# Weight set-up in pieces beside the first groups' stages, and order lists of their own for the filling and emptying steps

## The chip, the cores and the metric

One core of one Trainium2 chip. The metric is the time of one execution on the device in microseconds (us). Every time below is of the kernel before, from its runs or from one profiled execution of it.

## The reference

128 graphs of 64 nodes with 256 features pass four layers, each followed by a residual sum and a layer norm. With `x` the running features and `adj` the adjacency of a graph:

```python
# layer 0: hypergraph convolution, twice (W1: 256 -> 512, W2: 512 -> 256)
H = (adj != 0); w = adj[first row]
conv(x, W, b) = 1/(H @ w) * (H @ (1/colsum(H) * (H.T @ (x @ W.T)))) + b
h = layer_norm(relu(conv(x, W1, b1)), gamma, beta)
x = LN(x + conv(h, W2, b2) + x)
# layer 1: q, k = split(x @ Wqk1); w = rowsum(q * (adj @ (k * mask))) / 16
x = LN(x + softmax(w * mask over nodes) * (x @ Wv1))
# layer 2: 8 heads of 32, scores * (adj + adj), softmax, Wo, biases
x = LN(x + attention(x; Wq, bq, Wk, bk, Wv, bv, Wo, bo))
# layer 3: gate = sigmoid(rowsum(adj) * Wd + bd); xg = x * gate
QK = sigmoid(xg @ Wqk3.T + bqk); s = QK @ QK.T / 16 * adj; a = s / rowsum(s)
x = LN(x + relu((a @ xg) @ Wl.T + bl + xg @ Wr.T))
```

## The kernel before, in words

The 8192 rows of `x` are cut into 32 groups of 256 (4 graphs, two tiles of 128 rows). Every product with a float32 operand is made from two float16 parts, high and low, by three matmuls (`mm3`, lines 460 to 462: hi·hi, hi·lo, lo·hi). ScalarE (ACT) casts the high part, VectorE (DVE, `low`, line 898) or GpSimd (POOL, `sub`, line 1202) makes the low part by subtraction.

**The pipeline.** The work on a group is cut into six streams, `stream0` to `stream5` on each engine: 0 and 1 are layer 0, 1 and 2 layer 1, 2 to 4 layer 2, 4 and 5 layer 3. In step s, stream k works on group s − k. There are 37 steps: steps 0 to 5 fill the pipeline (written out), steps 6 to 31 have all six streams (a loop of two steps a turn), steps 32 to 36 empty it (written out). Each stream is a Python generator that yields after each piece of work. `run` (lines 271 to 289) takes, for each engine, one list written out by hand or by a planner (`ORDER_PE`, `ORDER_ACT`, `ORDER_DVE`, `ORDER_POOL`, lines 44 to 47): entry k lets stream k emit its next piece. So a list is the fixed order in which one engine does the pieces of the six streams in a step; engines wait for each other only by semaphores, and each does its own list strictly in order. In filling and emptying steps the same list is used, and entries of streams that have no group are skipped.

**Names of pieces** used below, with the lines of the matmuls or instructions. PE: `wt` (turn of the layer 1 weights, 595), `W2a` and `W2b` (the product with W2 for tile 0, last piece of stream 0, and for tile 1, first of stream 1), `md` (hypergraph matrix and degree, 519 to 525), `z1`, `zA`, `zB` (product with W1 in two halves), `rsum` (sums for the layer norm, 556 to 560), `conv2`, `x1t`, `x2t`, `xgt` (turns of x1, x2, xg, 485), `u` (product with Gm), `k`, `v`, `q`, `sc0`, `sc1` (scores, 638), `et0`, `et1` (turns of the exponentials, 649), `ctx0`, `ctx1` (662), `o` (product with Wo), `qk3`, `y3`, `s3`, `o2`, `rowsum` (706, 707), `o1` (layer 3). DVE: `HT` (964) and `cnt` (967) begin stream 0, `HBh`, `HBl`, `Pl`, `z1l`, `rFl1` (1006), `rmean`, `rmm`, `rvar` (1009 to 1015) end it; `y0` (1023), `Sm1`, `mx1` (1104, 1109), `SA` (1159), `preF` (1137), `stF` (954), `ssum` (1169), `o3` (1179). ACT: `xC`, `xF` (norms, 739), `exp0`. POOL: `xl`, `y0l` (1202), `preG` (1312), `xg` (1301). In the trace `late` is the name of two large buffers that hold the staged weights first, then x3, x4, Sm, Ssb, cx, gw, xg, o2 and o3.

**The set-up.** Before any stream begins, the eleven weights are loaded, split and partly combined: SyncE (SP) issues W2, the twelve small inputs, W1 and the nine other weights, and after them the first group's `x` and adjacency (`load_conv`, `load_layer1`), one queue in order. DVE clears its buffers, waits for W2 and all small inputs, scales W2 by gamma, centres it by column sums from PE, and makes the low parts of all eleven weights; ACT casts the high parts; PE makes two sums over W2, the product Gm of the two halves of Wqk1, and bv·Wo, and then waits until all eleven are split (`unstaged`) before its first stream piece. The eleven weights are staged in `late0`, `late1`, `r` and `rsq`.

```python
            pe.wait_ge(ev("unstaged"), len(weights_in))   # PE, ahead of its streams
...
            pool.wait_ge(ev("unstaged"), len(weights_in)) # POOL, ahead of its streams
...
            def step(j, s, lo, hi):
                live = {k: streams[k](At(k, j, s)) for k in range(lo, hi + 1)}
                for k in order:
                    if k in live:
                        next(live[k], None)
```

PSUM banks are held from piece to piece: stream 0 works in bA (from `md` to the sums; the next group's `md` waits for `rvar`), layer 3 in bG (from `xgt` to `o1`; the next `xgt` waits for `o3`).

Of the kernel before, what the change touches and what calls it, by code (L numbers as in the profile page):

```python
# [43 lines left out]
ORDER_PE = [2, 1, 4, 3, 5, 0, 4, 2, 3, 2, 0, 5, 1, 4, 0, 2, 5, 3, 0, 0, 3, 1, 5, 4, 5, 1, 5, 3, 2, 3, 1, 0, 2, 0, 4]  # L44
ORDER_ACT = [0, 4, 3, 1, 5, 2, 0, 5, 0, 3, 5, 4, 0, 4, 4, 5, 1, 0, 0, 0, 1, 0, 0, 0, 3, 2, 1, 3, 2, 5, 4, 3, 2, 4, 5]
ORDER_DVE = [0, 0, 4, 0, 0, 2, 0, 2, 0, 1, 0, 4, 0, 4, 0, 4, 3, 5, 4, 0, 2, 2, 1, 5, 1, 3, 1, 0, 2, 5, 2, 3, 2, 4, 3, 3, 3, 1, 5, 0, 4, 5, 4, 5, 4, 1, 5, 2, 3, 1, 5, 5, 0, 1, 0, 3, 2, 4, 0]
ORDER_POOL = [0, 0, 0, 1, 1, 0, 4, 3, 1, 1, 1, 1, 5, 2, 2, 3, 2, 0, 3, 0, 4, 0, 4, 4, 5, 4, 5, 5, 5, 0, 0, 0]
# [4 lines left out]


def build(nc, x, adj, adj_t, mask, mask_col, w1t, b1, gamma, beta, w2t, b2, wqk1t, wv1, wqt, bq, wkt, bk, wvt, bv,
          wot, bo, wqk3t, bqk, wlt, bl, wrt, wd, bd, out):
    ctx = ExitStack()
    with ctx:
# [28 lines left out]
        def weight(name, chunks, n):  # L86
# [28 lines left out]
                  "Wqk3": r[:, 0:2], "Wl": r[:, 2:4], "Wr": rsq[:, 0:2]}  # L115
# [103 lines left out]
        g2 = sb("g2", [P, TILES, D])  # L219
        xgFh = sb("xgFh", [P, 2, TOK], F16)  # L220
# [88 lines left out]
        def _(sp):  # L309
# [82 lines left out]
            def stage_in(i):  # L392
# [4 lines left out]
            small = [(gam[:], gamma), (bet[:], beta),  # L397
                     (wdb[:], wd.rearrange("(o d) -> o d", o=1).broadcast_to([P, D])),
# [958 lines left out]
```

## Time and profile before

| what | us |
|---|---|
| median of 3 runs | 1034.5 |
| lowest, highest run | 1030.52, 1379.15 |
| the profiled execution | 1032.15 |
| its span, first to last instruction | 1030.4 |
| mean granted TensorE clock in it (share of full) | 0.962 |

The span is a little shorter than the execution's time; what is between them, 1.75 us, lies outside the instructions. One run of the three was 1379.15 us; the other two and the profiled execution lie within 4 us of each other.

### The profile page before, as it was taken

Reading aid. Unit: us, or ns where it says so; the run is one execution under the profiler, and the core shown is the slowest. Engines: PE = TensorE matmul, PEld = TensorE weight load, DVE = VectorE, ACT = ScalarE, POOL = GpSimd, SP = SyncE. Lnnn points to the kernel's source line nnn. Section 1 sums busy time; section 2 is a strip of 40 time slices with the busy share of each in tenths; the row PEclk is TensorE's granted clock in tenths of the full one; section 3 lists DMA queues with packets and bytes.
Section 4 is the critical chain, followed back from the end, with each engine's and each line's share of the span. In section 5 each row is a group of like instructions: output and inputs, shape, how many; then the busy total and the mean of one; then the engine's idle time right before and its main releaser. Section 6 shows DMA issues by size and latency. Waiting matters only on the chain.

```text
span 1030.4 us, 32446 instructions
## 1 busy us (share of the span) xinstructions
PE 939.0 (91%) x11228; PEld 817.9 (79%) x11228; DVE 851.3 (83%) x2503; ACT 723.2 (70%) x1516; POOL 753.2 (73%) x1163
## 2 busy tenths in 40 slices
PE   3477899999999999999999999999999999998854
PEld 2356778888888888888888888888888888887642
DVE  4335789999999999999999999999999999987742
ACT  2234577787777787777877777887777777776542
POOL 3245678888888888888888888888888888875541
PEclk9579999999999999999999999999999999999975
DMA  7100222222222222222222221222222222211100
GB/s 212 32 27 8 59 60 62 71 71 69 68 56 66 55 58 56 67 59 69 69 69 66 56 65 53 57 59 69 59 69 69 69 64 62 53 45 39 49 14 20
DMA packets 110231, 61.80 MB, mean 60 GB/s; under 512 B 57072, under 2 KB 105840, under 8 KB 110192
## 3 DMA queue, kind: packets, MB, share of 16 engines
q1 hardware_dynamic: 110192, 61.30, 22.8%
q8 instruction: 22, 0.36, 0.1%
q14 instruction: 17, 0.14, 0.0%
HBM read 35.83 MB, written 8.39 MB: 43 GB/s over the span
## 4 chain that ended last, share of the span: by engine, by line
PE 72%; DVE 17%; ACT 4%; POOL 2%; issue 2%; DMA 1%; SPq 1%; POOLq 0%; ACTq 0%; DVEq 0%
PE bank L460 19%; PE bank L462 17%; PE bank L461 17%; PE bank L638 4%; PE bank L485 4%; DVE rFl L1006 4%; PE bank L662 3%; PE bank L649 2%; DVE Smx L1109 2%; DVE late L1104 2%; DVE late L1164 2%; DVE preF L1137 2%; DVE x1Fl L898 1%; PE bank L560 1%; PE bank L530 1%
## 5 line engine op out<-in xcount | busy, mean ns | idle before, releaser
L460 PE MATMUL bank<-z1h,W 128*128 128x256 f16 x256 | 71.7, 280 | 3.4 <-DVE z1l L898 3.3
L461 PE MATMUL bank<-z1l,W 128*128 128x256 f16 x256 | 71.4, 279 | 0.0
L462 PE MATMUL bank<-z1h,W 128*128 128x256 f16 x256 | 71.4, 279 | 0.0
L461 PE MATMUL bank<-W,rFh 128*128 128x256 f16 x256 | 71.0, 277 | 0.0
L462 PE MATMUL bank<-W,rFl 128*128 128x256 f16 x256 | 71.0, 277 | 0.0
L460 PE MATMUL bank<-W,rFh 128*128 128x256 f16 x256 | 70.9, 277 | 0.0
L1289 POOL TENSOR_TENSOR late<-late,Smx 128x512 f32<-128x512 f32 x64 | 67.8, 1060 | 2.4 <-DVE Smx L1109 1.7
L766 ACT ACTIVATE r<-bank,b1c 128x256 f32<-128x256 f32 x128 | 52.7, 465 | 8.7 <-PE bank L462 7.5
L1219 POOL TENSOR_TENSOR gp<-late,bdb 128x512 f32<-128x512 f32 x32 | 52.8, 1650 | 6.2 <-ACT late L846 6.2
L1104 DVE TENSOR_TENSOR late<-bank,acD 128x512 f32<-128x512 f32 x64 | 43.8, 684 | 14.7 <-PE bank L638 14.6
L1244 POOL TENSOR_TENSOR rsq<-rsq 128x512 f32<-128x512 f32 x32 | 52.8, 1650 | 2.2 <-ACT rsq L774 2.2
L1150 DVE SCALAR_TENSOR_TENSOR Ql<-qt,Qh 128x512 f16<-128x512 f32 x32 | 35.6, 1111 | 20.9 <-ACT Qh L873 20.7
L1202 POOL TENSOR_TENSOR rFl<-r,rFh 128x512 f16<-128x512 f32 x32 | 37.2, 1162 | 19.2 <-ACT rFh L723 19.2
L739 ACT ACTIVATE late<-preG,nbG,rsG 128x256 f32<-128x256 f32 x64 | 35.0, 594 | 21.9 <-POOL nbG L1214 21.9
L485 PE MATMUL bank<-ident,late 128*128 128x128 f32 x256 | 40.5, 282 | 10.6 <-POOL late L1301 10.4
L1006 DVE TENSOR_TENSOR rFl<-r,rFh 128x512 f16<-128x512 f32 x32 | 43.4, 1357 | 8.1 <-ACT rFh L723 8.1
L638 PE MATMUL bank<-Kbd,qh 128*64 128x256 f16 x512 | 46.9, 278 | 2.4 <-DMA Kbd<-kst 2.4
L1207 POOL TENSOR_SCALAR veB<-mvB 128x2 f32<-128x2 f32 x32 | 7.0, 219 | 54.7 <-DVE mvB L959 54.7
L723 ACT ACTIVATE SAh<-SA 128x256 f16<-128x256 f32 x32 | 13.4, 417 | 47.2 <-DVE SA L1159 47.1
L835 ACT ACTIVATE E<-late 128x512 f32<-128x512 f32 x64 | 39.9, 623 | 8.7 <-POOL late L1289 8.7
L739 ACT ACTIVATE late<-preF,nbF,rsF 128x256 f32<-128x256 f32 x64 | 35.0, 593 | 15.3 <-POOL nbF L1214 15.1
L954 DVE BATCH_NORM_STATS2 stG<-preG 128x6 f32<-128x256 f32 x64 | 24.1, 419 | 25.6 <-POOL preG L1312 25.6
(286 smaller groups left out, 4625.9 us busy)
## 6 DMA issues: line engine op xcount, KB each, us to landing
Vbd<-vst SPq DMA_DIRECT2D x128, 66.0 KB, 2.1
xin<-x SPq DMA_DIRECT2D x32, 256.0 KB, 2.7
xres<-x SPq DMA_DIRECT2D x32, 256.0 KB, 2.8
Kbd<-kst SPq DMA_DIRECT2D x128, 64.0 KB, 2.0
out<-late SPq DMA_DIRECT2D x32, 256.0 KB, 2.2
mrow<-mask SPq DMA_DIRECT2D x32, 128.0 KB, 3.1
atA<-adj_t SPq DMA_DIRECT2D x64, 32.0 KB, 2.3
aC<-adj SPq DMA_DIRECT2D x64, 32.0 KB, 2.1
```

The costliest lines, as they stand in the source:

```text
L460: pe.matmul(o, sh, mh, start=start, stop=False, skip_group_check=True)
L461: pe.matmul(o, sh, ml, start=False, stop=False, skip_group_check=True)
L462: return pe.matmul(o, sl, mh, start=False, stop=stop, skip_group_check=True)
L485: m = pe.transpose(o[:, c * TOK + t * P:c * TOK + (t + 1) * P], src[:, t, c * P:(c + 1) * P], ident_[:])
L638: m = pe.matmul(o[64 * b:64 * b + 64, c * 256:(c + 1) * 256], qq[:, c, tok], Kbd[:, :, hl, c, tok], start=(i == 0), stop=(i == 2), skip_gr ...
L739: m = act.activation(dst[:, t], pre[k][:, t], ACT.Identity, bias=nb[k][:, t:t + 1], scale=rs[k][:, t:t + 1])
L766: m = act.activation(r[:, 2 * i + c], (bA, bB)[i][:, c * TOK:(c + 1) * TOK], ACT.Relu, bias=b1c[:, 2 * i + c:2 * i + c + 1], scale=1.0 / WS)
L1006: dve.tensor_tensor(rFl[:, 2:4], r[:, 2:4], rFh[:, 2:4], ALU.subtract).then_inc(ev("rF_lo1"), 1)
L1104: dve.tensor_tensor(Sm[:, t], (bD0, bD1)[t][:].rearrange("p (h k) -> p h k", h=HEADS), acD[:, at.par, t:t + 1].broadcast_to([P, HEADS, NOD ...
L1219: return pool.tensor_tensor(dst, src, b[:].rearrange("p (o d) -> p o d", o=1).broadcast_to([P, TILES, D]), ALU.add)
L1244: pool.tensor_tensor(rsq[:, 0:2], rsq[:, 0:2], rsq[:, 2:4], ALU.add).then_inc(ev("sq_sum"), 1)
L1289: pool.tensor_tensor(Ssb[:, t], Sm[:, t], Smx[:, t:t + 1].rearrange("p t h -> p h t").broadcast_to([P, HEADS, NODES]), ALU.subtract).then_ ...
```

## The change

The set-up becomes a seventh stream (number 6, `set_up` on each engine), whose pieces stand in the lists of steps 0 to 3. Steps 0 to 5 and 32 to 36 get lists of their own (`HEAD_*`, `TAIL_*`); the lists of the loop (`ORDER_*`) are changed too. SP issues W1, the first group's `x` and adjacency, gamma, beta, b1, W2, Wqk1 and Wv1, the other small inputs, the first group's layer 1 inputs, and then the seven other weights. The general waits ahead of the streams go; each piece that needs a weight waits for that weight's count of `unstaged`, for group 0 alone. Wqk3, Wl and Wr are staged in gp, gt and o3r, the sums over W2 go to banks bF0 and bF1 and bv·Wo to bG. The clearing of Kbd, Vbd and vst on POOL is cut into nine pieces.

In names of pieces (S for a set-up piece; `Sx` on ACT and DVE is the high or low part of weight x), the lists that the text below speaks of; "was" is what the old list leaves of itself in that step:

```text
PE   loop  was  wt W2b ctx0 k qk3 md ctx1 wback v wsum Pt y3 conv2 cxt z1 v1 s3 sc0 zA zB sc1 x1t o2 o rowsum u o1 et0 x2t et1 uxT rsum q W2a xgt
           now  k wt W2b qk3 md wback ctx0 ctx1 v wsum y3 conv2 Pt v1 z1 cxt sc0 s3 zA zB sc1 x1t o2 o rowsum u et0 x2t o1 et1 uxT rsum q W2a xgt
PE   step 0 was md Pt z1 zA zB rsum W2a
           now  md Pt z1 zA zB S(sum) S(beta) S(Gm) rsum W2a
DVE  step 0 was HT cnt cnt1 be HBh HBl Dbg Dd Dinv Pl z1l rFl1 rmean rmm rvar
           now  HT cnt cnt1 be HBh HBl Dbg Dd Dinv Pl S(copy) S(scale) SW1 z1l S(beta) S(centre) S(c2) rFl1 SW2 rmean S(small) rmm rvar
ACT  step 1 was xh y0h Pf Ph z1h xB relu0 relu1 rFh0 x1Fh sq0 rFh1 sq1 uh
           now  SW2 xh y0h Pf SGm SWv1 Ph SWq z1h xB relu0 relu1 rFh0 x1Fh sq0 rFh1 sq1 uh
DVE  loop  was  ... mx1 x1Fl o2 rFl1 preF ssum stF srec mvF ul o3 ...
           now  ... mx1 x1Fl o2 preF rFl1 stF ssum mvF srec ul o3 ...
PE   step 35 was ctx0 qk3 ctx1 y3 cxt s3 o2 o rowsum o1 xgt
           now  ctx0 ctx1 qk3 cxt y3 o s3 o2 rowsum o1 xgt
DVE  step 35 was deg ri0 cx0 ri1 Ql cx1 y3l SA cFl o2 preF ssum stF srec mvF o3 stG mvG xgFl
           now  deg ri0 cx0 ri1 cx1 cFl Ql y3l preF SA stF mvF o2 ssum srec o3 stG mvG xgFl
POOL step 35 was gp SAl veF rsF nbF preG xg veG rsG nbG
           now  gp veF SAl rsF nbF xg preG veG rsG nbG
```

```diff
+HEAD_PE = [[0, 0, 0, 0, 0, 6, 6, 6, 0, 0], [1, 0, 0, 1, 0, 0, 0, 1, 1, 1, 0, 0], ...
...
+SETUP = LAST_LAG + 1
...
             def step(j, s, lo, hi, order):
                 live = {k: streams[k](At(k, j, s)) for k in range(lo, hi + 1)}
+                if j is None and s <= LAST_LAG:
+                    live[SETUP] = pieces
                 for k in order:
-                    if k in live:
-                        next(live[k], None)
+                    next(live[k], None)
...
             for s in range(first):
-                step(None, s, 0, s)
+                step(None, s, 0, s, head[s])
...
             for s in range(last, STEPS):
-                step(None, s, max(0, s - GROUPS + 1), LAST_LAG)
+                step(None, s, max(0, s - GROUPS + 1), LAST_LAG, tail[s - last])
...
-            stage_in(1)
+            stage_in(0)
+            sp.wait_ge(ev("const"), 2)
+            load_conv(At(0, None, 0))
+            for dst, src in ((gam[:], gamma), (bet[:], beta), (b1c[:], b1)):
+                sp.dma_start(dst, src).then_inc(ev("w2_in"), 16)
+            stage_in(1)
+            for i in range(2, 4):
+                stage_in(i)
             for dst, src in small:
                 sp.dma_start(dst, src).then_inc(ev("small_in"), 16)
-            stage_in(0)
-            for i in range(2, len(weights_in)):
+            load_layer1(At(0, None, 0))
+            for i in range(4, len(weights_in)):
                 stage_in(i)
-            sp.wait_ge(ev("cleared"), 1)
-            load_conv(At(0, None, 0))
-            load_layer1(At(0, None, 0))
...
-            pe.wait_ge(ev("unstaged"), len(weights_in))
+            pe.wait_ge(ev("ident"), 3)
+
+            def set_up():
+                pe.wait_ge(ev("setup"), 2)
+                for k in range(4):
+                    m = pe.matmul(bF0[:, 0:D], onesf[:], w2_stage[:, k, 0:D], start=(k == 0), stop=(k == 3))
+                m.then_inc(ev("setup_pe"), 1)
+                yield
...
+            def first_needs(at, k):
+
+                if not at.earlier(1):
+                    pe.wait_ge(ev("unstaged"), k)
...
+            dve.memset(atA[:], 0.0).then_inc(ev("const"), 1)
+            dve.memset(aC[:], 0.0).then_inc(ev("const"), 1)
...
+                dve.wait_ge(ev("w2_in"), 64)
+                dve.tensor_copy(w2_stage[:, :, D:2 * D], w2_stage[:, :, 0:D]).then_inc(ev("setup"), 1)
...
-            for part, value in ((Kbd[:], 0.0), (Vbd[:], 0.0), (vst[:, 1], 0.0), (vst[:, 0], 1.0)):
-                pool.memset(part, value).then_inc(ev("ident"), 1)
-            pool.wait_ge(ev("unstaged"), len(weights_in))
+            def set_up():
+                for h in range(4):
+                    pool.memset(Kbd[:, h], 0.0).then_inc(ev("ident"), 1)
+                    yield
...
```

## Rows read from the trace of the kernel before

**Rows 1.** The page: PE busy, then its busy tenths in 40 slices

```profile
PE 939.0 (91%) x11228; PEld 817.9 (79%) x11228; DVE 851.3 (83%) x2503; ACT 723.2 (70%) x1516; POOL 753.2 (73%) x1163
...
PE   3477899999999999999999999999999999998854
```

**Rows 2.** Windows, one a step: length, busy us by engine, PEclk, DMA

```profile
29.22:50.44 21.22, 9.41 (x71) 7.18 (x72) 5.50 (x18) 5.88 (x13) 4.71 (x8) 0.58 0.15 38
50.44:75.67 25.23, 17.89 (x130) 13.09 (x128) 9.15 (x31) 8.57 (x18) 10.55 (x18) 0.70 0.09 27
75.67:99.12 23.45, 18.31 (x170) 14.69 (x169) 12.84 (x45) 10.82 (x24) 12.09 (x22) 0.93 0.04 10
99.12:123.77 24.65, 20.69 (x226) 17.02 (x225) 17.81 (x53) 14.28 (x31) 15.73 (x25) 1.00 0.25 61
123.77:150.26 26.49, 24.86 (x316) 20.58 (x316) 22.12 (x66) 18.05 (x39) 19.69 (x31) 1.00 0.23 59
...
178.69:207.08 28.39, 28.19 (x361) 25.05 (x354) 26.06 (x77) 22.27 (x49) 23.43 (x37) 1.00 0.26 65
907.30:934.58 27.28, 25.17 (x300) 21.94 (x300) 22.73 (x64) 17.26 (x34) 19.30 (x31) 0.94 0.15 38
...
977.84:997.78 19.94, 13.11 (x134) 9.97 (x134) 9.92 (x27) 10.04 (x19) 7.29 (x13) 0.83 0.06 18
```

**Rows 3.** DMA issues to 60 us: count, KB each, median us to landing

```profile
late<-w2t SPq DMA_DIRECT2D x1, 512.0 KB, 4.0
late<-w1t SPq DMA_DIRECT2D x1, 512.0 KB, 6.3
...
atA<-adj_t SPq DMA_DIRECT2D x8, 32.0 KB, 3.0
```

**Rows 4.** Timeline of DVE: start, us, instruction, [idle before <-releaser]

```profile
12.64 0.69 DVE L922 COPY late<-late 128x1024 f32<-128x1024 f32 x1 [9.34 <-DMA bvc<-bv]
...
17.01 1.23 DVE L898 SCALAR_TENSOR_TENSOR W<-late,W 128x1024 f16<-128x1024 f32 x1 [1.30 <-ACT W L723]
...
28.90 0.29 DVE L964 TENSOR_SCALAR HT<-atA 128x256 f16<-128x256 f32 x1
...
37.74 0.69 DVE L898 SCALAR_TENSOR_TENSOR z1l<-bank,z1h 128x512 f16<-128x512 f32 x1 [2.18 <-ACT z1h L723]
...
54.80 0.88 DVE L1023 SCALAR_TENSOR_TENSOR y<-bank,rsc,c 128x256 f32<-128x256 f32 x2 [2.43 <-PE bank L462]
```

**Rows 5.** Timeline of PE, set-up and around the end of step 0

```profile
17.98 1.89 PE L496 MATMUL bank<-late,betb 128*128 128x256 f32 x8
...
48.19 0.16 PE L556 MATMUL bank<-ones,rFh 128*128 128x1 f16 x1 [5.36 <-POOL rsq L1247]
...
49.48 0.37 PE L460 MATMUL bank<-W,rFh 128*128 128x256 f16 x1
...
54.34 0.42 PE L462 MATMUL bank<-W,rFl 128*128 128x256 f16 x1
```

**Rows 6.** Timeline of POOL, set-up

```profile
1.57 3.51 POOL L1198 MEMSET Kbd<- 128x4096 f16 x1
```

**Rows 7.** Waits of PE in the loop (170 to 850 us): total, times, longest

```profile
PE bank L460 <- DVE ssum L1169: 2.3, 11, 0.2
```

**Rows 8.** Timeline of ACT in one step of the loop

```profile
225.35 1.08 ACT L739 ACTIVATE x<-preC,nbC,rsC 128x256 f32<-128x256 f32 x2
```

**Rows 9.** Timeline of DVE in the same step

```profile
226.69 0.14 DVE L1169 TENSOR_SCALAR ssum<-bank 128x2 f32<-128x2 f32 x1
226.81 0.75 DVE L954 BATCH_NORM_STATS2 stF<-preF 128x6 f32<-128x256 f32 x2
```

**Rows 10.** Timeline of DVE in step 35

```profile
997.17 0.69 DVE L1137 SCALAR_TENSOR_TENSOR preF<-bank,x2b 128x512 f32<-128x512 f32 x1 [0.62 <-PE bank L462]
...
998.98 0.88 DVE L1179 SCALAR_TENSOR_TENSOR late<-bank,srec,late 128x256 f32<-128x256 f32 x2
```

**Rows 11.** Timeline of POOL in step 35

```profile
1002.21 1.26 POOL L1301 TENSOR_TENSOR late<-g,late 128x512 f32<-128x512 f32 x1
```

More of the change, by code:

```diff
@@ L219, in build @@
         g2 = sb("g2", [P, TILES, D])
+        for name, buf in (("Wqk3", gp), ("Wl", gt), ("Wr", o3r)):
+            stages[name] = buf[:]
         xgFh = sb("xgFh", [P, 2, TOK], F16)
@@ L762, in stream0 @@
                     act.wait_ge(ev("y0_raw"), at.n(-1))
+                if not at.earlier(1):
+                    act.wait_ge(ev("w2_in"), 64)
                 def relu(i):
@@ L824, in stream3 @@
                 yield
+                if not at.earlier(1):
+                    act.wait_ge(ev("ident"), 13)
                 act.wait_ge(ev("v"), at.n())
@@ L843, in stream4 @@
             def stream4(at):
+                if not at.earlier(1):
+                    act.wait_ge(ev("small_in"), 16 * SMALL_INPUTS)
                 act.wait_ge(ev("deg"), at.n())
@@ L851, in stream4 @@
                 yield
+                if not at.earlier(1):
+                    act.wait_ge(ev("unstaged"), len(weights_in))
                 act.wait_ge(ev("gate_pre"), at.n())
@@ L1092, in stream3 @@
             def stream3(at):
+                if not at.earlier(1):
+                    dve.wait_ge(ev("ident"), 13)
                 dve.wait_ge(ev("k_hi"), at.n())
@@ L1196, in _, with set_up @@
             pool.wait_ge(ev("ident"), 3)
-            for part, value in ((Kbd[:], 0.0), (Vbd[:], 0.0), (vst[:, 1], 0.0), (vst[:, 0], 1.0)):
-                pool.memset(part, value).then_inc(ev("ident"), 1)
-            pool.wait_ge(ev("unstaged"), len(weights_in))
+            def set_up():
+                for h in range(4):
+                    pool.memset(Kbd[:, h], 0.0).then_inc(ev("ident"), 1)
+                    yield
+                for par in range(2):
+                    for b in range(2):
+                        pool.memset(Vbd[:, par, b], 0.0).then_inc(ev("ident"), 1)
+                        yield
+                for part, value in ((vst[:, 1], 0.0), (vst[:, 0], 1.0)):
+                    pool.memset(part, value).then_inc(ev("ident"), 1)
+                yield
             def sub(dst, a, b):
@@ L1259, in stream1 @@
             def stream1(at):
+                if not at.earlier(1):
+                    pool.wait_ge(ev("setup"), 5)
                 pool.wait_ge(ev(f"xres_in{at.par}"), at.dma(1))
@@ L1281, in stream3 @@
                     pool.wait_ge(ev("preF"), at.n(-2))
+                if not at.earlier(1):
+                    pool.wait_ge(ev("unstaged"), 8)
                 pool.wait_ge(ev("xC"), at.n())
@@ L1293, in stream4 @@
             def stream4(at):
+                if not at.earlier(1):
+                    pool.wait_ge(ev("unstaged"), 9)
                 pool.wait_ge(ev("gate_scaled"), at.n())
```

194 lines of the change are left out of this document (116 added, 78 removed).

## The prediction

> **What bounds the kernel now.** I read the page first, then windows of one step each, then the timelines of the stretches where the windows show idle time. The page has PE busy 939.0 of 1030.4 us, and its 40 slices show where it is not: the first four and the last five [rows 1]. The windows put sizes to this [rows 2]. Their bounds are the starts of `cnt` (DVE), once a step, and at the end those of `ssum`. A step of the loop takes 28.39 us with PE busy 28.19: 26 such steps, 738 us, are bound by PE, and no order can give back more than 0.2 × 26 = 5.2 us there. The filling steps 0 to 4 take 21.22, 25.23, 23.45, 24.65 and 26.49 us with PE busy 9.41, 17.89, 18.31, 20.69 and 24.86; they are chains of small pieces, each engine waiting for another. The emptying steps are alike: 27.28 us with 25.17 busy in step 32, 19.94 with 13.11 in step 35. Ahead of all this the first `HT` starts at 28.90 us [rows 4]: by then the whole set-up has been done and no group's work but one cast of `x`.
>
> **The start.** In the new order W1 is issued first, at the time at which W2 is now, 0.74 us; W2 landed 4.0 us after its issue [rows 3], so W1 is there at 4.7. SP then waits for two memsets that end by about 1.8 us and issues `x` (some 0.5 us) and two adjacency blocks (some 0.65 each), the last by 3.8; such blocks land 3.0 us after issue [rows 3], at 6.8. `HT` starts there in place of 28.90 [rows 4]: −22.1 us. Bounds: if the block lands as late after issue as W1 does now under load, 6.3 us [rows 3], it is 10.1 and the gain 18.8; on the other side issues half a us quicker than I count give 22.6.
> The trace shows one load of 512 KB taking 4.0 us on an idle queue and 6.3 on a full one [rows 3]. The Trainium skill (DMA: Bandwidth & Descriptors, Queues, rings and completion order) says that a transfer's semaphore write lands only after every earlier write of the same DMA engine. By that rule the group's blocks come after all of W1, which speaks against putting W1 ahead of them; here it would hold `HT` to W1's landing, and by the row for an idle queue that is already past at 4.7.
>
> **Step 0 with set-up pieces in it.** DVE now sits idle 2.18 us ahead of `z1l` [rows 4]. Three pieces go there: the copy (0.69), the scaling (about 1.1) and W1's low part (1.23) [rows 4], about 3.0 us: `z1l` comes 0.8 late, and with it `zA`, `zB`. W2 must have landed when the copy starts, 37.74 − 2.18 − 22.1 = 13.5 us; it is issued at about 5.5 and lands 4.0 to 6.3 later [rows 3], in time by 1.7 us or more. PE waits 5.36 us between `zB` and `rsum` [rows 5], and gets three pieces of eight matmuls; one such piece is 1.89 busy [rows 5], 5.2 to 5.7 together, which fit to 0.3 us. The scaling of small inputs ahead of `rmm` delays `rvar` by about 0.5. Cost: +1.3 us.
>
> **PE's clock.** The same pieces may bring something. In step 0 the granted clock was 0.58 in the mean and in step 1 0.70 [rows 2], that is the lower level (1.2 GHz) for most of it. `W2a` and `W2b`, 24 matmuls, ran from 49.48 to 54.34 [rows 5], 0.21 us apart, after the 5.36 us of idling; at the upper level they would be half that, −2.5 us. With PE busy in that gap I take the upper level for them. `y0` (54.80 [rows 4]) waits for `W2b`, but also for DVE's `HBl`, which is itself 1.3 late and would then be last: of −2.5 and +1.3 together there remains −1.1 us. The rest of step 1 has 36 matmuls of the same kind in its chain, worth up to −3.6 us, nothing if the clock falls back in the gaps; I take −1, nearer to nothing, as the 0.70 was granted with the same gaps.
>
> **Steps 1 to 3 with set-up pieces.** ACT gets ten casts, DVE ten pieces, POOL seven of the nine memsets (the whole of Kbd took 3.51 us [rows 6], so about 0.9 each), PE one short piece. A low part of 512 columns is 0.69 (`z1l`, the same shape [rows 4]); the cast of 512 columns is no more than a norm of as many, 1.08 [rows 8]. That is up to 11 us of ACT and 7 of DVE in three steps in which they are busy 33.7 and 39.8 of 73.3 us [rows 2]. In the idle stretches they cost nothing; where one stands ahead of a piece of the chain it costs its length. Between 0 and +7, I take +2: the casts `SGm` and `SWv1` stand between `Pf` and `Ph`, and PE's turn hides one of them.
>
> **The filling steps' own lists.** For PE, step 1 keeps its order. In steps 2 to 4 `q`, `v` and the score pieces move. PE idles 5.1, 4.0 and 1.6 us there [rows 2], 10.7 together, which bounds the gain; `cnt` to `rvar` is a chain through one bank that no list shortens. I take a third, −3.5, bounds −8 and +2.
>
> **The loop's lists.** PE waits for `ssum` ahead of `o1` (2.3 us in 11 steps of 24, 0.2 at most [rows 7]). The new list puts `et0` and `x2t` between: 0.9 us of work ahead of the wait, while DVE puts `stF` (0.75 [rows 9]) ahead of `ssum`. I take half of the bound of 5.2: −2.5 us; on the other side the next rival but one.
>
> **The emptying steps' lists.** In step 35 `preF` starts at 997.17 and `xg` ends at 1003.5, and only then can PE go on [rows 10, 11]. Now `o` stands ahead of `s3` and `preF` ahead of `SA`: about 4 us earlier; POOL does `xg` ahead of `preG`: 1.26 earlier [rows 11]. What is late next is bank bG, free when `o3` ends, 998.98 + 0.88 − about 0.7 [rows 10] = 999.2: −4.1 us. Steps 32 to 34 keep more of their order, with 2.1 us of PE idle in step 32 [rows 2]; I take 1 each. Sum −7, bounds −3 and −12. Step 36 has one stream and no order to change.
>
> **Sum.** −22.1 + 1.3 − 2.4 (W2 product; with the 1.3 this is the −1.1) − 1 + 2 − 3.5 − 2.5 − 7 = −35.2. On the profiled execution's own 1032.15 us: 997.0. That execution lies 2.35 us under the median of the three runs; I put half of it back: 998 us.
>
> **The rivals.**
> *Only the start is gained.* The pieces eat what the clock gives, and the lists move idle time without shortening a chain: −22.1 + 1.3 − 1.1 + 2 = −20, so 1012. For it: the chains of steps 0 and 1 keep their order. Against it: 4 us of step 35 can be read off piece by piece.
> *The lists bring more.* −8 in the filling steps, −5 in the loop, −11 in the emptying, −3 for the clock: 985. For it: PE's idle times are that large. Against: banks bA and bG.
> *The loop gets worse; slower than before.* `x2t` now stands ahead of `o1`, and everything behind it on PE, `o1`, `et1`, `uxT`, waits with it for `xC`. `xC` ends at 226.43 [rows 8]; `x2t` would start at about 227.05, 0.6 us later. If ACT reaches `xC` more than 0.6 us later than now, each further us costs 26. At 2.5 us late it is 1.9 × 26 = 49, so 998 + 2.5 + 49 = 1050; from 1.9 us late on the loss, 1.3 × 26 = 34 us, outweighs all that is gained. Against: the new ACT list has `xC` one piece earlier.
> *The loads don't do what the order says.* `x` and its blocks wait behind what is issued after them, and `HT` starts near 12: 1003.
>
> **Chances.** Forecast 0.55, by itself 990 to 1007; only the start 0.20; more 0.15; late loads 0.05; worse loop 0.05. A measurement of this kernel can tell about 2% from no change, here 1013.8. The first, third and fourth are faster, and of the second somewhat more than half (it lies 2 us under that bound): 0.55 + 0.15 + 0.05 + 0.12 = 0.87; within 2% 0.09; slower 0.04. The range 985 to 1013 leaves out half of the third, a third of the second and the last: under 0.2.
>
> **What would show it.** `HT` at 6.5 to 7.5 us; `z1l` near 16.4; `W2a` with matmuls 0.11 us apart and `y0` near 31.6; step lengths of steps 1 to 4 together under 99.8 − 2; the loop's step between 28.2 and 28.4; `xg` of step 35 ahead of `preG`. It is wrong if the loop's step is over 28.6, if DVE's wait ahead of the copy shows W2 landing after 13.5, or if the filling steps grow by as much as the start gained.

## The result and the profile after

The changed kernel takes 1002.55 us (median of 4 runs, 999.49 to 1005.13), the kernel before 1033.2 beside it (4 runs, the 1379.15 among them): ratio 0.9713, 95% interval 0.9672 to 0.9753, that one run left out. The forecast was 998, with 985 to 1013. The profiled execution took 999.49 us, span 997.7 (before: 1032.15 and 1030.4).

The page of the changed kernel: busy time by engine, then PE's busy tenths and its granted clock in 40 slices.

```profile
PE 928.4 (93%) x11228; PEld 812.0 (81%) x11228; DVE 836.6 (84%) x2503; ACT 702.5 (70%) x1516; POOL 746.0 (75%) x1169
...
PE   4687899999999999999999999999999999999854
...
PEclk9779999999999999999999999999999999999995
```

The first slice has work in it now, where [rows 1] had 3 tenths. The second thing to see is that PE has 10.6 us less of busy time for the same 11228 matmuls; so its busy time is not work alone, which matters below.

Windows of the changed kernel, cut as in [rows 2]: steps 0 to 4, one of the loop, then 32, 35 and 36.

```profile
6.72:29.99 23.27, 15.64 (x101) 12.31 (x102) 13.05 (x37) 6.93 (x14) 4.97 (x7) 1.00 0.77 231
29.99:53.58 23.59, 16.09 (x120) 11.83 (x118) 10.21 (x33) 9.49 (x20) 14.14 (x22) 0.71 0.10 29
53.58:78.14 24.56, 19.75 (x171) 16.20 (x170) 15.40 (x46) 14.44 (x31) 15.04 (x26) 0.87 0.04 9
78.14:104.56 26.42, 20.98 (x269) 17.81 (x269) 21.77 (x60) 14.31 (x32) 16.46 (x26) 1.00 0.23 57
104.56:131.17 26.61, 22.92 (x266) 20.08 (x259) 21.98 (x64) 17.18 (x38) 19.19 (x30) 1.00 0.24 58
...
161.58:189.47 27.89, 27.89 (x350) 24.77 (x349) 25.32 (x79) 21.03 (x46) 23.04 (x35) 1.00 0.25 66
882.77:904.50 21.73, 21.59 (x276) 19.14 (x274) 18.99 (x62) 13.78 (x30) 15.36 (x26) 1.00 0.12 33
...
949.03:966.97 17.94, 12.06 (x134) 9.41 (x134) 11.39 (x32) 10.06 (x20) 9.01 (x15) 0.90 0.07 20
966.97:986.72 19.75, 11.15 (x62) 7.17 (x62) 5.27 (x14) 5.88 (x11) 5.26 (x10) 0.65 0.04 13
```

Against [rows 2]: the loop's step is 0.5 us shorter in this window, steps 32 and 35 are 5.5 and 2.0 shorter, step 0 is 2.1 longer, and steps 1 to 4 together are 101.18 us where they were 99.82; the prediction wanted them under 97.8. Step 1 is granted 0.71 of the clock, where it was 0.70. The granted clock of step 0, 1.00, says less than it seems: the trace's clock records begin only at 22.7 us, and the matmuls ahead of that, shown below, still run at the lower level.

The span splits at three marks on DVE: the first `HT`, the first `rmean` (end of step 0's chain), and the `rmean` of steps 6 and 31. The table has this for every kernel that speaks to the lists (us; "new" names the lists that are those of the change).

```text
kernel       new lists    first HT   to rmean   rmean 0 to 6   loop step   rmean 31 to end   span
before       none          28.90      20.75       154.82        28.358        116.99        1030.4
start_only   none           6.12      22.22       156.40        28.342        112.10        1005.4
loop_old     fill, empty    6.19      21.74       153.39        28.358        111.83        1002.1
tail_old     fill, loop     5.93      22.18       151.36        27.974        120.57         999.4
head_old     loop, empty    5.98      22.50       153.21        27.974        112.17         993.2
after        all            6.38      22.55       155.67        28.047        111.93         997.7
```

The loop's column is the mean of 25 steps. A step is cut at `rmean`, which the new loop list has 2.7 us earlier in the step (23.06 us behind `cnt` where it was 25.74); with that list the filling stretch reads 2.7 us shorter and the last stretch 2.7 longer. From before to after: −22.5 at the start, +1.8, +0.85, −7.8 in the loop, −5.1 at the end, −32.7 in all.

**The start came as forecast.** DVE of the changed kernel in steps 0 and 1:

```profile
6.38 0.31 DVE L1035 TENSOR_SCALAR HT<-atA 128x256 f16<-128x256 f32 x1 [3.10 <-DMA atA<-adj_t]
...
13.20 0.68 DVE L980 COPY late<-late 128x1024 f32<-128x1024 f32 x1
...
16.11 0.68 DVE L951 SCALAR_TENSOR_TENSOR z1l<-bank,z1h 128x512 f16<-128x512 f32 x1
...
31.84 0.87 DVE L1094 SCALAR_TENSOR_TENSOR y<-bank,rsc,c 128x256 f32<-128x256 f32 x2
```

`HT` was forecast at 6.8 (the block's landing, which is 6.27 in the trace), `z1l` at 16.4, `y0` at 31.6. The copy of W2 starts at 13.20 with no wait for its load. PE of the changed kernel, from `zB` to W2's product:

```profile
21.59 0.42 PE L482 MATMUL bank<-z1l,W 128*128 128x256 f16 x1
21.80 0.42 PE L483 MATMUL bank<-z1h,W 128*128 128x256 f16 x1
22.01 2.21 PE L516 MATMUL bank<-late,onesf 128*128 128x256 f32 x8
24.07 1.89 PE L521 MATMUL bank<-late,betb 128*128 128x256 f32 x8
25.79 1.89 PE L527 MATMUL bank<-late 128*128 128x256 f32 x8
...
28.79 0.28 PE L481 MATMUL bank<-W,rFh 128*128 128x256 f16 x1
28.91 0.27 PE L482 MATMUL bank<-W,rFh 128*128 128x256 f16 x1
29.01 0.27 PE L483 MATMUL bank<-W,rFl 128*128 128x256 f16 x1
```

The three set-up pieces fill what was a gap of 5.36 us [rows 5]. Ahead of them matmuls start 0.21 us apart, behind them 0.11: the lower level (1.2 GHz) has given way to the upper (2.4 GHz) once PE was busy without a gap, as forecast. It did not last: in step 1 the granted clock is 0.71 again.

**The loop gained more than was thought possible.** PE around `o1`; first the kernel before:

```profile
226.50 0.27 PE L462 MATMUL bank<-x1Fh,Gm 128*128 128x256 f16 x1
226.89 0.28 PE L460 MATMUL bank<-y3h,SAh 128*128 128x256 f16 x1
```

and the changed kernel, in another step of its loop:

```profile
518.47 0.27 PE L483 MATMUL bank<-x1Fh,Gm 128*128 128x256 f16 x1
518.58 0.60 PE L688 MATMUL bank<-ident,E 128*128 128x128 f32 x4
519.02 0.60 PE L506 MATMUL bank<-ident,x 128*128 128x128 f32 x4
519.46 0.27 PE L481 MATMUL bank<-y3h,SAh 128*128 128x256 f16 x1
```

Where PE is not held, a matmul starts 0.11 us after the one ahead of it, though each is shown busy for 0.27: neighbours overlap. Before, the next one came 0.39 later, 0.28 lost, and the profile could show only what the 0.27 did not cover, 0.12 of idle time. Over the 25 steps of the loop these gaps, less 0.11 each, add up to 7.9 us, and the idle time in them to 3.9: read by starts the loss is twice what it is read by busy time. The weight loads' wait reads higher still, 10.6 us in 24 steps, and that is more than was lost by starts and more than the 9.5 us that the loop later gave back; the waits of PE's weight loads in the loop of the kernel before:

```profile
PEld bank L460 <- DVE ssum L1169: 10.6, 24, 0.5
```

In the changed kernel that wait is gone. The Trainium skill (Perfetto Trace Analysis, Identifying the Most-Contended Engine) says that PE's matmul busy share is not a good measure of how close a kernel is to roofline, because pipelined instructions look smaller in the trace, and names the weight loads' busy share as one that is. The rows here agree that matmul busy time misleads: 2.3 us of waiting on matmuls [rows 7] (2.5 in the longer window of this row) against 7.9 by starts. They differ in that a matmul here looks longer than its spacing (0.27 against 0.11), and in that the weight loads' 10.6 is not exact either.

### The profile page after: what moved, and what is told of

It is laid out like the page before. It is cut to its first block and busy times, and to the rows that moved or that the text cites. A ratio compares the mean times of both kernels' runs of the same rounds, so it can differ in the third digit from the quotient of the medians.

```text
span 997.7 us, 32479 instructions
## 1 busy us (share of the span) xinstructions
PE 928.4 (93%) x11228; PEld 812.0 (81%) x11228; DVE 836.6 (84%) x2503; ACT 702.5 (70%) x1516; POOL 746.0 (75%) x1169
## 5 line engine op out<-in xcount | busy, mean ns | idle before, releaser
L1300 POOL TENSOR_TENSOR gp<-late,bdb 128x512 f32<-128x512 f32 x32 | 40.7, 1271 | 32.7 <-ACT late L897 32.7
L1283 POOL TENSOR_TENSOR y0l<-y,y0h 128x512 f16<-128x512 f32 x32 | 37.2, 1163 | 31.6 <-ACT y0h L766 31.6
L766 ACT ACTIVATE z1h<-bank 128x512 f16<-128x512 f32 x32 | 19.1, 598 | 50.2 <-PE bank L483 50.2
L784 ACT ACTIVATE x<-preB,nbB,rsB 128x256 f32<-128x256 f32 x64 | 34.9, 593 | 22.0 <-POOL nbB L1295 22.0
L951 DVE SCALAR_TENSOR_TENSOR PTl<-bank,PTh 128x512 f16<-128x512 f32 x64 | 43.6, 681 | 2.6 <-ACT PTh L766 2.6
L1399 POOL TENSOR_TENSOR preG<-o3r,late 128x512 f32<-128x512 f32 x32 | 40.8, 1274 | 6.4 <-ACT o3r L937 5.6
L481 PE MATMUL bank<-Wv,x2Fh 128*128 128x128 f16 x256 | 44.8, 220 | 0.0
L483 PE MATMUL bank<-Wv,x2Fl 128*128 128x128 f16 x256 | 44.5, 219 | 0.0
L482 PE MATMUL bank<-Wv,x2Fh 128*128 128x128 f16 x256 | 44.5, 219 | 0.0
```

The source lines that it names most:

```text
L481: pe.matmul(o, sh, mh, start=start, stop=False, skip_group_check=True)
L482: pe.matmul(o, sh, ml, start=False, stop=False, skip_group_check=True)
L483: return pe.matmul(o, sl, mh, start=False, stop=stop, skip_group_check=True)
L784: m = act.activation(dst[:, t], pre[k][:, t], ACT.Identity, bias=nb[k][:, t:t + 1], scale=rs[k][:, t:t + 1])
L951: return dve.scalar_tensor_tensor(out=dst, in0=src, scalar=scale, in1=hi, op0=ALU.mult, op1=ALU.subtract)
L1283: return pool.tensor_tensor(dst, a, b, ALU.subtract)
```

## The experiments

**The loop's lists put back.** The four `ORDER_*` lists as before, all else as changed.

```diff
-ORDER_PE = [3, 2, 1, 5, 0, 2, 4, 4, 3, ...      # and ACT, DVE, POOL
+ORDER_PE = [2, 1, 4, 3, 5, 0, 4, 2, 3, ...
```

> The changed kernel with the four lists of the loop as they were; lists of the filling and emptying steps stay new. Theory A (the loop gained 0.31 us a step by the new lists): the step from one `cnt` to the next is 28.36 again and the whole is 8 us longer than the changed kernel, about 1010. Theory B (my sum: at most 0.2 us a step could be gained, 2.5 us in all): 2 to 3 us longer, about 1005. If the time is the same, the loop's gain came with the state in which the filling steps leave the queues.

Measured: 1005.26 us (1003.88 to 1006.58), ratio 0.975 [0.9721, 0.9779]; loop step 28.358, to the last digit that of before. All of the loop's gain is in those four lists, 0.38 us a step against a steady 27.974.

**The emptying lists put back.** `TAIL_*` is the old loop list, with absent groups left out.

> The changed kernel with steps 32 to 36 in the old manner, the old loop's lists with absent streams left out. Theory A (my sum): +7 us, of it 4.1 in step 35 (`xgt` waits for `xg`, made after `preG`). Rival, by the last `rmean` to the end in the two traces, 116.99 against 111.93: +5. Second rival (what the chain of a bank sets, lists can't change): 0.

Measured: 1000.95 us (999.76 to 1003.96), ratio 0.9709 [0.9675, 0.9743]: no loss in the median, though its last stretch is 8.6 us longer than in the changed kernel. The other stretches make up for it: rmean 0 to 6 is 4.3 shorter, the loop 1.8. The lists of those stretches are the same in both kernels, so these 6.1 us are not the edit's.

**The filling lists put back.** `HEAD_*` is the old order, each set-up piece behind the piece that it follows now.

> The changed kernel with steps 0 to 5 in the old order of the six streams; each set-up piece stands behind the same piece as in the new lists. Theory A (my sum): the new lists gave 3.5 us, so +3.5, about 1006. Theory B: from the first `rmean` to the one of step 6 both traces take the same (155.67 now, 154.82 before), so the new lists gave nothing and the set-up pieces cost nothing: 0. Theory C: the pieces cost 5 or more there and the new lists are what hides them: +5 or more.

Measured: 997.15 us (994.26 to 999.47), ratio 0.9673 [0.9634, 0.9711]. The filling lists bring nothing; by the medians they cost 5 us. In the profiles 1.8 of it is the loop, whose lists were not touched, and 2.5 the filling stretch, at a different granted clock (step 1 0.77 for 0.71, step 2 0.93 for 0.87).

**The set-up pieces made short.** Of Wq, Wk, Wv, Wo, Wqk3, Wl and Wr only two columns are cast and split; the rest of them is filled with a constant ahead of the first group, so that the output is another.

> The changed kernel, in which the casts and low parts of Wq, Wk, Wv, Wo, Wqk3, Wl and Wr are made of 2 columns in place of 512 (the weights are filled with a constant ahead of the first group, so that the output is another). It leaves out 7 casts of about 0.6 us on ACT and 7 low parts of 0.7 us on DVE in steps 1 to 3. Theory A (my sum): they cost 2 us, so steps 1 to 3 get 1 to 2 us shorter. Theory B (they lie in idle time): 0. Theory C (they ate the gain of the lists): 4 us or more shorter.

Measured: 1007.06 us (1004.08 to 1008.96), ratio 0.9754 [0.9722, 0.9786]. The fills hold the first `HT` to 10.94, which is 4.6 of it. The stretch of steps 0 to 6 took 153.06 us, inside the spread of kernels with full pieces (151.4 to 155.7): the pieces' length doesn't show there. (POOL's memsets and W1, W2, Wqk1 and Wv1 are whole in it.) But the loop's step was 28.344 in place of 28.05, and every second one 28.85. DVE and POOL of this kernel in a fast step:

```profile
532.52 0.61 DVE L957 SCALAR_TENSOR_TENSOR HBl<-HT,be,HBh 128x128 f16<-128x128 f16 x2
...
532.89 1.38 POOL L1315 TENSOR_TENSOR xres<-xres,b2b 128x512 f32<-128x512 f32 x1
```

and in the slow one after it:

```profile
560.38 1.63 DVE L957 SCALAR_TENSOR_TENSOR HBl<-HT,be,HBh 128x128 f16<-128x128 f16 x2
...
560.52 1.34 POOL L1315 TENSOR_TENSOR xres<-xres,b2b 128x512 f32<-128x512 f32 x1
```

`HBl` has two instructions (x2) of 0.35 us with two SBUF inputs. In the slow step POOL's addition starts while the first of them is under way, and the second then lasts until the addition is over: 1.63 us in place of 0.61. In the fast one the addition starts 0.37 us after `HBl`, with the second already begun. PE waits for `HBl` up to 0.8 us, 12 times, 9.3 us in the loop. The changed kernel has the same, more seldom; of the waits of PE's matmuls in its loop this is the one row:

```profile
PE bank L551 <- DVE HBl L951: 2.0, 2, 1.1
```

and the two steps in which it stands are 28.92 and 28.88 us long, from one `cnt` to the next, where the others are near 27.97. One and the same loop ran with the long step in every second place here, in two places in the changed kernel, and in none with the filling or emptying lists put back: the loop can run with either phase of the two engines, and what comes ahead of it sets which. That is worth 1.8 us between those kernels and the changed one. Whether it is also why the changed kernel's runs spread over 5.6 us is not shown, as none of its runs near 1005 us was profiled. For it speaks that these two runs had a mean granted clock of 0.980 and the two near 1000 us one of 0.977, so the clock did not make them slow.

**`HBl` taken out of POOL's way.** In DVE's loop list `wmx` and `wrm` go behind `HBl`, which so starts earlier.

```diff
-HT wmx cnt cnt1 wrm be HBh HBl ...
+HT cnt cnt1 be HBh HBl wmx wrm ...
```

> The changed kernel; in the loop DVE does `wmx` and `wrm` behind `HBl` in place of ahead of it, so that `HBl` starts about 0.4 us earlier and is under way before POOL starts its 1.3 us addition `xres`. Theory A (where POOL's addition starts first, `HBl` takes 1.63 us in place of 0.61 and PE waits 0.8 us in every second step, in some runs): all steps 27.9 to 28.1, no run near 1005, median near 999. Theory B (the runs near 1005 have another cause, such as the clock in steps 0 to 2): the runs still differ by 5 us.

Measured: 995.32 us (993.79 to 996.13), ratio 0.9647 [0.9624, 0.967]. No step of the loop over 28.3, 27.968 in the mean, `HBl` at most 0.352 us an instruction (1.358 in the changed kernel), and all runs within 2.3 us. The median is 7.2 us under the changed kernel, but one move of two small pieces has not earned all of that. The two profiled executions are 4.7 us apart: 2.0 in the loop, which is where the move is, 4.0 between the `rmean` of step 0 and of step 6 and 0.4 ahead of it, less 1.7 in the last stretch. The filling lists are the same in both kernels. What differs there is the granted clock; steps 1 and 2 of this kernel, to be held against the second and third window of the changed one:

```profile
29.57:52.26 22.69, 15.18 (x124) 11.10 (x122) 10.13 (x34) 9.50 (x20) 14.14 (x22) 0.77 0.11 30
52.26:73.86 21.60, 16.50 (x167) 13.87 (x166) 14.07 (x46) 14.45 (x31) 15.05 (x26) 1.00 0.06 11
```

Four kernels have the same filling lists, whole pieces and no added matmuls (us; steps from `cnt` to `cnt`):

```text
kernel       clock of steps 1, 2   step 1   step 2   steps 0 to 5
after        0.71, 0.87            23.59    24.56       154.86
hb_first     0.77, 1.00            22.69    21.60       150.71
tail_old     0.84, 0.92            21.28    22.38       150.18
loop_old     0.84, 0.92            21.06    22.39       149.02
```

The same order of the same pieces takes up to 5.8 us more where the lower level is granted for longer; whether the waits or the clock come first, these rows don't say. A difference of a few us between two medians can be this and not the edit.

**Two of the loop's edits alone, on the kernel before.** First PE's: `o1` goes behind `et0` and `x2t`.

```diff
-... uxt ... rowsum u o1 et0 x2t et1 ...
+... uxt ... rowsum u et0 x2t o1 et1 ...
```

> The kernel before with the PE edit alone. `et0` then follows `u` and waits for `preF`, which DVE still makes behind `rFl1` and just ahead of `ssum`. Theory A (both lists are needed): the step stays within 0.1 us of 28.36. Rival (the PE edit alone moves work into the wait): 28.05, as with both.

Measured: 1034.94 us (7 runs), ratio 1.0032 [1.0004, 1.006]; step 28.446. `et0` now waits for `preF` (which reads the bank that `et1` fills next), and `preF` stands behind `rFl1` on DVE: the weight loads of `et0` stand 10.5 us in 24 steps, as long as those of `o1` did before. Then DVE's edits with it: `rFl1 preF ssum stF srec mvF ul` becomes `preF rFl1 stF ssum mvF srec ul`.

> The kernel before with two edits alone: on PE `o1` stands behind `et0` and `x2t`, on DVE the stretch `rFl1 preF ssum stF srec mvF ul` becomes `preF rFl1 stF ssum mvF srec ul`. Theory A (all of the loop's gain is PE's wait for `ssum` ahead of `o1`, 0.31 us a step): the step goes from 28.36 to 28.05 and the whole gets 8 us shorter. Theory B (the gain is spread over many places of the lists): under 0.1 us a step, at most 3 us.

Measured: 1046.5 us (1043.45 to 1047.67), ratio 1.0148 [1.0127, 1.0169]; step 28.922. The two edits that the prediction reasoned about make the kernel before slower by 15 us. Its DVE and POOL in one step:

```profile
225.64 0.69 DVE L1137 SCALAR_TENSOR_TENSOR preF<-bank,x2b 128x512 f32<-128x512 f32 x1 [0.60 <-PE bank L462]
226.25 1.40 DVE L1006 TENSOR_TENSOR rFl<-r,rFh 128x512 f16<-128x512 f32 x1
227.57 0.74 DVE L954 BATCH_NORM_STATS2 stF<-preF 128x6 f32<-128x256 f32 x2
228.23 0.14 DVE L1169 TENSOR_SCALAR ssum<-bank 128x2 f32<-128x2 f32 x1
...
225.82 1.28 POOL L1244 TENSOR_TENSOR rsq<-rsq 128x512 f32<-128x512 f32 x1
```

and those of the changed kernel:

```profile
517.37 0.69 DVE L1210 SCALAR_TENSOR_TENSOR preF<-bank,x2b 128x512 f32<-128x512 f32 x1 [0.55 <-PE bank L483]
517.98 0.68 DVE L1077 TENSOR_TENSOR rFl<-r,rFh 128x512 f16<-128x512 f32 x1
518.58 0.74 DVE L1025 BATCH_NORM_STATS2 stF<-preF 128x6 f32<-128x256 f32 x2
519.24 0.14 DVE L1242 TENSOR_SCALAR ssum<-bank 128x2 f32<-128x2 f32 x1
...
517.99 1.80 POOL L1325 TENSOR_TENSOR rsq<-rsq 128x512 f32<-128x512 f32 x1
```

The order on DVE is the same, the length of `rFl1` is not: 1.40 where POOL's `rsq` began 0.43 us ahead of it, 0.68 where it began 0.01 behind, and then it is `rsq` that is long, 1.80 for 1.28. PE waits 0.54 us for `ssum` in the one and not at all in the other. By all 23 or 24 of the loop, `rFl1` on DVE is 1.45 us before, 1.47 here and 0.68 after (medians). Whoever starts first goes on nearly undisturbed, and the other is held up.

**POOL's list too.** The same kernel with POOL's new loop list.

> The kernel before with the PE and DVE edits that made its step 28.92, and now the new loop list of POOL as well. Theory A (what the two edits lacked is that DVE's `rFl1`, 1.40 us beside POOL's additions and 0.68 without, starts before POOL's `rsq`): `rFl1` 0.68 us in the median, step 28.05 to 28.1, the whole 7 to 9 us under the kernel before. Theory B (ACT's list, or the whole of the new lists, is needed): `rFl1` stays near 1.4 and the step over 28.5.

Measured: 1124.42 us (1119.49 to 1125.93), ratio 1.0885 [1.0846, 1.0924], step 31.71. The theory that POOL's list is all that was missing falls: `rFl1` has a median of 1.11 us, and PE now waits most for ACT, here in the loop:

```profile
PE bank L602 <- ACT wex L801: 28.4, 21, 1.4
```

ACT still has the old order, and so have all other places of PE's and DVE's lists; which of these makes `wex` late, and so the step long, no run here parts. What is shown is that PE's edit alone, PE's with DVE's, and these two with POOL's list gain nothing, and that the four whole lists together gain 0.38 us a step. The lists of DVE, POOL or ACT alone were not run.

**PE kept busy in the first steps.** On the changed kernel, matmuls of a constant (`ident` by `onesf`) into unused columns of a bank, read by no one: 20 ahead of step 0, then 3 to 7 ahead of the waits for p_f, p_lo, z1_lo, x1F_lo and u_lo in steps 0 to 2.

```diff
+def keep_busy(at, stream, n):
+    if at.j is None and at.fixed + stream <= WARM_STEPS:
+        o = bF1 if at.fixed + stream == 2 else bD1
+        for _ in range(n):
+            pe.matmul(o[:, D:D + P], ident[:], onesf[:], start=True, stop=True)
```

> The changed kernel with matmuls of ident by onesf into a free bank, which no one reads, added where PE waits: 20 ahead of step 0, and 3 to 7 each ahead of the waits for `Pf`, `Pl`, `z1l`, `x1Fl` and `ul` in steps 0 to 2. Theory A (the lower clock is what makes steps 0 to 2 long, and PE's idle time is what lowers it): matmuls of 256 columns 0.11 us apart throughout, steps 0 to 2 together 4 to 6 us shorter, and the time differs less from run to run. Theory B (those steps are chains of waits in which PE's speed counts little): under 2 us. If the added matmuls hold up the work behind them it gets longer.

Measured: 991.97 us (989.7 to 992.63), ratio 0.9608 [0.9584, 0.9632]. Windows of 10 us of the changed kernel, and behind them of this one:

```profile
30.00:40.00 10.00, 6.14 (x51) 4.25 (x49) 6.40 (x20) 4.11 (x10) 8.12 (x15) 0.82 0.18 54
40.00:50.00 10.00, 6.41 (x34) 4.29 (x32) 1.40 (x3) 5.38 (x12) 5.98 (x7) 0.67 0.05 13
```

```profile
30.00:40.00 10.00, 8.41 (x76) 7.04 (x74) 3.55 (x10) 6.83 (x17) 8.73 (x13) 1.00 0.25 67
40.00:50.00 10.00, 8.57 (x96) 7.60 (x96) 7.23 (x29) 3.11 (x7) 6.20 (x11) 1.00 0.09 21
```

The third number from the end is the granted clock: 0.82 and 0.67 have become 1.00. Step 0 with the pieces is 3.0 us shorter to its `rmean`, from there to the next `rmean` another 4.4 (19.48 for 23.87). The median is 10.6 us lower, but that is not all the clock of these steps: the profile has 1.8 of it in the loop (27.974). Steps 0 to 5 take 147.96 us from `cnt` to `cnt`. That is 6.9 less than in the changed kernel, but only 1 to 3 less than in the three others of the table above, which got a better clock without help. So the added matmuls are worth 1 to 7 us here, by what the kernel beside them was granted.

**All that helped, together.** `HBl` first, PE kept busy in steps 0 and 1, and on SP `x` and its blocks ahead of W1.

> The changed kernel with three edits: `wmx` and `wrm` behind `HBl` in the loop, the added matmuls in PE's waits of steps 0 and 1 (none in step 2, where the step was 1.5 us longer with them), and `x` of the first group issued ahead of W1, which is cast behind it. Theory: -7 by the first, -4 by the second, up to -0.8 by the third (`HT` near 5.6 us if a transfer's arrival waits for what was issued ahead of it, unchanged at 6.0 if the adjacency's own issue and landing set it): 988 to 991. Rival (the gains overlap, since all the three take away waits of the same steps): 992 or more.

Measured: 988.66 us (988.53 to 990.74), ratio 0.9591 [0.9563, 0.9619]. The first `HT` starts at 4.87, against 5.93 to 6.38 where 512 KB of W1 are issued ahead of the blocks. Steps 0 to 5 take 144.32 us. The kernel with `HBl` first is 6.7 us above this one, the one with PE kept busy 3.3: the gains of the two overlap, since by themselves they had 7.2 and 10.6.

**The same, with PE kept busy in the last group too.** 24 more such matmuls, ahead of the last group's waits for xg, xgF_lo, qk_tanh, y3_lo and attn.

> As the one before, and added matmuls in PE's waits of the last group in steps 35 and 36 as well (24 of them). Theory A (the last chain is long by the lower clock: 36 matmuls of 256 columns 0.21 us apart in place of 0.11): from the start of `ssum` of group 30 to that of group 31 3 to 4 us less than 19.75, the whole 3 to 4 us less than without them. Rival (the clock doesn't rise by them, or they hold up the work behind): no gain.

Measured: 987.45 us (986.53 to 987.58), ratio 0.957 [0.9544, 0.9597]: some 44 us under the kernel before, 15 under the change, and so better than both. Windows in the last steps, of the kernel without these matmuls:

```profile
966.00:975.00 9.00, 6.80 (x36) 4.34 (x34) 2.03 (x4) 1.48 (x3) 0.67 (x1) 0.50 0.05 17
```

and with them:

```profile
966.00:975.00 9.00, 6.09 (x59) 4.92 (x58) 2.73 (x6) 3.46 (x7) 0.67 (x1) 1.00 0.09 29
```

The lower level all through without, the upper with, and step 36 is 16.49 us for 20.01. Of these 3.5 us only 1.2 arrive in the median; the profiled execution lost 1.0 up to the first `rmean` and 1.6 between the second and the third (23.65 for 22.03). The clock granted in step 2 is 0.86 in it and 0.92 in the other; why is open.

**Only the start.** The changed kernel with every list of pieces as before: the loads' order and the divided set-up are all that is left of the change.

> The changed kernel with every list of pieces in the order of the kernel before (filling, loop and emptying), so that of the change only the loads' order and the divided set-up remain. This is the rival 'only the start is gained', run by itself; it was forecast at 1012 on the median of before. Theory A (the loop's lists bring 8 to 10 us, the filling lists nothing, the emptying lists 4 to 8, the start 21 to 22): first HT at 5.9 to 6.5 us, loop's step 28.36 us, the stretch from the step after the loop's last rmean to the end of the span 117 to 121 us, filling stretch 151 to 156, median 1008 to 1014. Theory B (the three kinds of lists give nothing by themselves in sum, since each of e4, e5 and e6 lies within 5 us of the changed kernel): median 1000 to 1006. Theory C (the lists work only together: undoing one is cheap as the others make up for it): median over 1016, with a loop's step over 28.5.

Measured: 1008.12 us (1007.16 to 1015.75), ratio 0.9792 [0.9762, 0.9822], that is 21.5 us less than before (18.4 to 24.6). The first theory holds for the median, `HT` and the step (28.342), but not for the last stretch, which is 112.10 where it said 117 to 121. The second, that the lists give nothing in sum, is 2 us off: its upper end was 1006. All lists together bring 5.6 us by the medians, no more than the clock of the first steps can move.

## Why the forecast was right, and where it was not

**The start, −22.1: right.** −22.5 in the profile, −22.8 in the run with only the start. Step 0's +1.3 came as +1.5 to +1.8.

**Set-up pieces, +2: too low. The clock of step 1, −1: it comes and goes.** The run with only the start has the old lists and the pieces: 156.40 against 154.82 for rmean 0 to 6, +1.6, where W2's product, the clock and the pieces together said −2.4 − 1 + 2 = −1.4. By steps from `cnt` to `cnt`, step 1 is 3.5 us shorter (21.72 for 25.24, at a granted clock of 0.84 for 0.70), which is all that the first two terms said. In the changed kernel's own profile step 1 is granted 0.71, and is 1.6 shorter. Steps 2 and 3 of that run are 2.2 and 2.6 us longer than before (25.66 for 23.44, 27.30 for 24.66), so the pieces cost up to 4.8 us, within the stated bounds of 0 to 7. As the run with short casts takes no less there than the others (22.36 and 27.95), it is hardly the length of ACT's and DVE's pieces. In step 3 of the run with only the start one wait of PE is new, for `HBl`, as in the slow steps of the loop:

```profile
PE bank L551 <- DVE HBl L951: 1.4, 1, 1.4
```

One `HBl` is held up to 1.35 us there beside POOL; the kernel before has none over 0.36. The other 3.4 us stay open; a part may be the clock of step 2, 0.87 there for 0.93.

**W2's product, −2.4: the mechanism right,** the matmuls 0.11 us apart. With step 0's cost it leaves `y0` 0.4 us nearer to `HT` than before (25.46 for 25.90), where −1.1 was forecast: `y0` is at 31.84 for 31.6 though `HT` came 0.4 early.

**The filling lists, −3.5: wrong, near nothing.** From the run with only the start to the one with old loop lists the stretch is 3.0 us shorter with them, from the one with old filling lists to the changed kernel it is 2.5 longer. In the latter pair the granted clock between 30 and 70 us is lower (0.82, 0.67, 0.66, 0.83 in the changed kernel), and that is more than the order shows: with one and the same set of filling lists steps 0 to 5 took 149.0 to 154.9 us. The failed step was "I take a third" of PE's idle time: idle time in a chain of waits is no stock that an order can draw on, and the prediction had said of the chain through one bank that no list shortens it.

**The loop's lists, −2.5: mis-sized by a factor of three,** and by the step "no order can give back more than 0.2 × 26 = 5.2 us". Measured: 0.31 us a step in the changed kernel's profile, 0.38 in every kernel in its good phase, 8 to 10 us. The bound took PE's span less its busy time for all that PE loses. Between pipelined matmuls busy time covers up to 0.16 us of each wait, and the gaps ahead of `o1` alone were 7.9 us by starts. The reason given for the gain was right in place (the wait for `ssum` ahead of `o1`) and incomplete: with the two edits named, the kernel before is 15 us slower, since `ssum` is late by `rFl1`, whose length goes by whether POOL has begun.

**The emptying lists, −7: about right in the profile, by another way.** The last stretch is 5.1 us shorter as read, and 7.8 once the moved mark (2.7 us) is taken out. Of step 35's 4.1 us, 2.0 came. PE, ACT and POOL of the changed kernel there:

```profile
970.37 0.66 PE L506 MATMUL bank<-ident,late 128*128 128x128 f32 x4 [2.36 <-POOL late L1388]
...
967.87 1.09 ACT L784 ACTIVATE late<-preF,nbF,rsF 128x256 f32<-128x256 f32 x2 [3.07 <-POOL nbF L1295]
...
969.05 1.27 POOL L1388 TENSOR_TENSOR late<-g,late 128x512 f32<-128x512 f32 x1 [1.21 <-ACT late L784]
970.27 1.27 POOL L1399 TENSOR_TENSOR preG<-o3r,late 128x512 f32<-128x512 f32 x1
```

`xg` (L1388) is ahead of `preG`, as forecast, and PE waits 2.36 us for it where it waited 4.71. What is late next is not bank bG, as I had it: `xg` starts when ACT ends the norm of `preF`, and ACT waited 3.07 us for `nbF`, the end of POOL's chain of small pieces. The largest gain is in step 32, 5.5 us. Part of it is clock: the run with only the start has the old emptying lists, and takes 25.60 us for step 32 and 18.74 for step 36 where before took 27.28 and 21.63. Its last stretch is 112.10 us, level with the 111.83 of the kernel that has the same loop and the new emptying lists; between the kernel with old emptying lists and the changed one it is 120.57 against 111.93. So by themselves the lists are worth between 0.3 and 8.6 us, and some 5 us of the last stretch come and go with the granted clock; no pair of runs here settles it.

**The sum.** Forecast −35.2 on the profiled time, measured −32.7. The start gave 0.4 more, step 0 cost 0.5 more, the loop gave 5.3 more, and the stretch from step 0's `rmean` to step 6 was to be 4.9 shorter (2.4 and 3.5 and 1, less 2) and is 3 to 4 longer when the moved mark is taken out: 8 us missed there, mostly balanced by the loop. That these two met was luck, and the total would not have shown it. It hardly tells the rivals apart either: late loads were put at 1003, which is where the kernel came out, and `HT` at 6.38 alone refutes them; "only the start" was put at 1012 (its sum counts step 0's 1.3 us twice) and, run by itself, is at 1008.12, 5.6 us above the change. The worse loop did not come. The same edits of PE and DVE on the old lists do cost 0.56 us a step, but by the wait for `ssum`, 14.0 us in 24 steps, and not by the wait for `xC` that the rival named.

## What to carry to other kernels

Size what a reordering can give back by the starts of neighbouring matmuls, never by span less busy time: for one and the same wait the starts gave 7.9 us, the waits of the weight loads 10.6 and those of the matmuls 2.5, and 9.5 came back. Judge the order lists of all engines as one thing; a part of the change alone can be worse than what it replaces. Before an instruction of two SBUF inputs on DVE is placed, look at what POOL begins just then, since a lead of a hundredth of a microsecond decides which of them is long. And where chains of small pieces fill and empty a pipeline, first see what clock is granted: a few unread matmuls ahead of the waits gave 1 to 7 us here, and the new lists of the filling steps nothing. Before a difference of some us is put down to an edit, cut both profiles into stretches and see whether it lies where the edit is.

## What the hardware showed that was not expected

- DVE and POOL hold each other over whole instructions: DVE's `rFl1` 0.68 us or 1.40 to 1.54, the pair of `HBl` 0.61 or 1.63, POOL's `rsq` 1.28 or 1.80. The Trainium skill (GPSIMD Engine Reference, Key points) says that POOL shares its SBUF interfaces with VectorE and contends with DVE instructions with two SBUF inputs; `rFl1` and `HBl` are such instructions, and the trace agrees. The rows also show that the one which starts first goes through nearly undisturbed.
- The loop with the new lists ran in two phases, with steps of 27.97 us and of 28.34 in the mean, the second all through one run only, and what happens in the first steps sets which it runs in.
- PE's granted clock in steps 1 to 3 and 32 to 36 differs between kernels with the same lists there: step 1 at 0.71, 0.77 or 0.84, and up to 5.8 us of time in the first steps and some 5 at the end.
- The first group's blocks land 1.1 to 1.5 us earlier if they are issued ahead of a load of 512 KB: `HT` at 4.87. The Trainium skill (DMA: Bandwidth & Descriptors, Queues, rings and completion order) has each semaphore write land only after the earlier writes of its DMA engine. No run here shows that rule at work: W1 lands at 4.33 us in the changed kernel, past as forecast when the two blocks land at 5.69 and 6.27, yet they take 3.1 to 3.3 us from issue where they take 2.0 to 2.2 ahead of it. `x`, issued between them, takes 4.0 us for 2.7. The other 0.4 us is that the blocks are issued that much earlier.
- A `cnt1` of two columns took 1.13 us (0.17 in other steps) where POOL's `xl` of 1.15 us began 0.05 ahead of it.
